# SyncE's order in the second entrance: slot 0's row and the fourth stack ahead of the second unit's writes, and the transposed maxima between two heads

## The reference

```
x = x + 0.5 * L0_ffn(ln(x)); x = x + L0_attn(ln(x)); x = x + 0.5 * L0_ffn(ln(x))
x = x + 0.5 * L1_ffn(ln(x)); x = x + L1_attn(ln(x)); x = x + 0.5 * L1_ffn(ln(x))

L1_attn: c_kv = x @ W_dkv.T ;  q = (x @ W_dq.T @ W_uq.T), 16 heads, times k_eff
         attn = softmax(causal(q_lat . c_kv / sqrt(8))) ;  y = (attn . c_kv) . v_eff
```

## Time and profile before

| what | value |
|---|---|
| median of 3 runs | 448.95 us (448.35 to 449.26) |
| the profiled execution: its own time | 450.93 us |
| its span in the profile | 448.8 us |
| TensorE busy | 404.5 us, 90% of the span |
| VectorE, ScalarE, GpSimd busy | 78%, 64%, 66% |
| DMA | 31.82 MB, mean 71 GB/s |

### The profile page before, as it was taken

One profiled execution on the slowest core, in us unless ns is written; L12 is line 12 of the kernel. 1 busy time (PEld: TensorE's weight loads), 2 busy tenths in 40 slices (PEclk: granted clock), 3 DMA queues, 4 the chain that ended last, 5 costly groups with the idle time before them and its releaser, 6 DMA issues.

```text
span 448.8 us, 11209 instructions
## 1 busy us (share of the span) xinstructions
PE 404.5 (90%) x3802; PEld 262.1 (58%) x3802; DVE 348.4 (78%) x878; ACT 286.1 (64%) x523; POOL 295.2 (66%) x557
## 2 busy tenths in 40 slices
PE   7999789999999998888879788879999999887996
PEld 2555436666666654444457564557777777545674
DVE  5888787887878866997799987747788888277992
ACT  6785525666676676787896447226558686778641
POOL 5524646777687772346999646346787789779962
PEclk9999999999999999999999999989999999999999
DMA  7001877332324200000000006895444331000001
GB/s 219 3 0 29 211 209 216 88 106 61 100 71 98 56 4 1 2 0 2 0 2 0 1 1 156 168 239 137 108 111 105 99 82 46 6 0 1 23 25 47
DMA packets 31124, 31.82 MB, mean 71 GB/s; under 512 B 4954, under 2 KB 26330, under 8 KB 31075
## 3 DMA queue, kind: packets, MB, share of 16 engines
q1 hardware_dynamic: 31074, 31.18, 27.3%
HBM read 21.30 MB, written 9.44 MB: 68 GB/s over the span
## 4 chain that ended last, share of the span: by engine, by line
PE 43%; DVE 20%; POOL 18%; issue 9%; ACT 5%; DMA 3%; SPq 1%; DVEq 0%; POOLq 0%; ACTq 0%
PE psum L725 5%; POOL hq L1523 4%; DVE nm L824 4%; PE psum L675 3%; POOL hb_v L1518 2%; POOL rstd L246 2%; PE psum L706 2%; PE psum L696 2%; PE psum L676 2%; PE psum L729 2%; DVE xn L240 2%; PE psum L678 2%; PE psum L697 2%; DVE stat L224 2%; PE psum L306 2%
## 5 line engine op out<-in xcount | busy, mean ns | idle before, releaser
L774 ACT ACTIVATE h_sb<-psum 128x1024 f32<-128x1024 f32 (+1 forms) x128 | 110.6, 914 | 54.1 <-PE psum L707 27.4
L824 DVE TENSOR_REDUCE nm<-psum 128x2 f32<-128x512 f32 x128 | 81.3, 683 | 11.9 <-PE psum L676 11.3
L827 DVE TENSOR_REDUCE nm<-psum 128x3 f32<-128x384 f32 x128 | 65.6, 551 | 15.4 <-PE psum L682 14.1
L784 POOL TENSOR_TENSOR h_sb<-h_sb,bandw 128x512 f32<-128x512 f32 x45 | 57.2, 1271 | 0.0
L246 POOL TENSOR_TENSOR rstd<-veps,mhalf 128x4 f32<-128x4 f32 (+1 forms) x25 | 26.2, 1049 | 43.7 <-DVE veps L232 43.2
L725 PE MATMUL psum<-h_sb,v_b 128*32 128x256 f32 x512 | 40.9, 391 | 3.9 <-POOL h_sb L788 2.1
L788 POOL TENSOR_SCALAR_AFFINE_SELECT h_sb<-h_sb 128x512 f32<-128x512 f32 x64 | 40.7, 637 | 0.0
L675 PE MATMUL psum<-kst,qst 72*128 72x256 bf16 x128 | 33.4, 278 | 3.2 <-DMA kst<-k_dram 1.4
L676 PE MATMUL psum<-kst,qst 72*128 72x256 bf16 x128 | 32.7, 272 | 0.0
L678 PE MATMUL psum<-kst,qst 72*128 72x128 bf16 x128 | 29.1, 228 | 2.5 <-DMA kst<-k_dram 1.8
L306 PE MATMUL psum<-h_sb,dw 128*64 128x256 f32 x256 | 30.9, 385 | 0.0
(11 more groups left out here) (256 smaller groups left out, 1144.4 us busy)
## 6 DMA issues: line engine op xcount, KB each, us to landing
qst<-q_dram SPq DMA_DIRECT2D x96, 96.0 KB
kst<-k_dram SPq DMA_DIRECT2D x96, 96.0 KB
q_dram<-q_parts SPq DMA_DIRECT2D x16, 192.0 KB, 3.0
k_dram<-k_parts SPq DMA_DIRECT2D x16, 192.0 KB, 2.9
k_dram<-k_parts SPq DMA_DIRECT2D x16, 128.0 KB, 3.2
x<-in_L_attn_x SPq DMA_DIRECT2D x4, 256.0 KB, 4.7
out_x<-x SPq DMA_DIRECT2D x4, 256.0 KB, 2.3
pk<-in_packed SPq DMA_DIRECT2D x1, 689.5 KB, 5.7
```

The source lines that it names most:

```text
L774: nc.scalar.activation(pexp[p][:, :, 0:w], psum[:, 4 + 2 * (p % 2):6 + 2 * (p % 2), 0:w], ACT.Exp, scale=scale).then_inc(sem("a_exp"), 1)
L784: ins = nc.gpsimd.tensor_tensor(wide, wide, bandw[:].unsqueeze(1).unsqueeze(1).to_broadcast([P, 2, 2, P]), ALU.mult)
L824: nc.vector.tensor_reduce(nm[slot % 2][:, HEAD[h]], bank[e].rearrange("p (t k) -> p t k", t=2), AX.X, ALU.max, negate=True).then_inc(sem(" ...
L827: nc.vector.tensor_reduce(nm3[slot % 2][:, HEAD[h]], bank[e][:, 0:3 * P].rearrange("p (t k) -> p t k", t=3), AX.X, ALU.max, negate=True).t ...
```

## The change

In the second entrance alone, SyncE no longer writes unit 1 ahead of row 0. It writes unit 1's first half behind stack 3, and its second half, then both halves of unit 2, then unit 3 behind row 1. In the second attention's front(1), TensorE's transposed maxima of slot 0 move from behind head 3 to between heads 2 and 3. For that `pe_scores` takes the heads of the pair that it is to do. The first layer's entrance keeps its order.

```
-            def pe_scores(pe, qd, slot, p, idle=0, b=6 if l0 else 5):
+            def pe_scores(pe, qd, slot, p, idle=0, b=6 if l0 else 5, which=range(2)):
...
-                for e in range(2):
+                for e in which:
...
                     for p in range(PR):
-                        pe_scores(eng, q0, slot, p, 1)
-                        if slot == 1 and p == 1:
+                        if slot == 1 and p == 1 and not l0:
+                            pe_scores(eng, q0, slot, p, 1, which=[0])
+                            pe_maxT(eng, q0, 0)
+                            pe_scores(eng, q0, slot, p, 1, which=[1])
+                        else:
+                            pe_scores(eng, q0, slot, p, 1)
+                        if slot == 1 and p == 1 and l0:
                             pe_maxT(eng, q0, 0)
...
                 at["prefetch"](eng, which)
-                run(ph, 3, 4 if which == "sp" else 5)
+                if which != "sp":
+                    run(ph, 3, 5)
+                elif ph is proj_a:
+                    run(ph, 3, 4)
...
                 elif which == "sp":
                     at["front"](eng, which, 0)
-                    ph["write"](eng, 2, [0])
+                    if ph is proj_a:
+                        ph["write"](eng, 2, [0])
+                    else:
+                        ph["write"](eng, 1, [0])
                     at["front"](eng, which, 1)
+                    if ph is proj_b:
+                        ph["write"](eng, 1, [1])
+                        ph["write"](eng, 2, [0])
                     ph["write"](eng, 2, [1])
                     ph["write"](eng, 3, [0, 1])
```

## The result

The changed kernel takes 455.92 us (median of 4 runs, 455.07 to 457.3) against 448.84 us of the kernel before: a ratio of 1.0161, 95% interval 1.0136 to 1.0186. The forecast was slower, 451.2 with a range up to 452.9. The side was right, the size was not: 7.1 us were lost where 2.2 were forecast.

What follows compares the result with a forecast made beforehand. TensorE was taken to bound the second attention. Unit 2 starting 0.9 us later for a late stack, plus 1.3 us of halved clock, made +2.2 us on the median of 448.95: 451.2 us, range 448.0 to 452.9.

Steps and rivals of the forecast that it cites:

- The bound: Second attention: TensorE is busy throughout, so its gains or losses before 308 us reach the end one to one.
- The row's wait goes: Second entrance: row 0, issued near 289.1, lands at 291.3, so TensorE's 2.46 us wait before slot 0's shifted scores goes.
- the sum: Whole kernel: unit 2 starts 0.9 us later and the clock costs 1.3, together +2.2 us, giving 451.2.
- rival A: Unit 2: the stack comes in time and the gain stands, 446.4 to 448.0 us; chance 0.12.
- The next transposition waits for the split: Second entrance: the second transposition needs slot 1's split and runs at 293.4 instead of 294.75, a gain of 1.35 us.
- The late stack: Unit 2: the next quad's stack, issued at 302.6, lands at 309.2 (308.3 to 310.3), starting the unit 0.9 us later.
- The clock: Behind unit 2's pause of 3.5 us TensorE's clock is halved, costing 1.3 us, bounds 0 and 1.7.
- Rivals B and A: B, a draw at unit 2: stack lands 308.3 to 309, 448.1 to 449.8 us, chance 0.2; A has its own line.
- Rival D: Second attention: row 1 or row 2 is late too, two pauses, up to +5 us; chance 0.08.

Runs made afterwards that it cites:

- e9: The kernel before, unchanged, run again for a second profile; ratio 1.0004 to the kernel before.
- e1: The kernel before with only the transposed maxima moved between heads 2 and 3, SyncE's order kept; ratio 0.998 to the kernel before.
- e2: The kernel before with only SyncE's new order, the transposed maxima staying behind head 3; ratio 1.0152 to the kernel before.
- e5: The whole change, but unit 1's six writes are issued by ScalarE on its own queue; ratio 0.9978 to the kernel before.
- e8: The whole change, but unit 1's first half is written ahead of row 0 again, its second where the first stood; ratio 1.0063 to the kernel before.
- e4: The whole change, but the writes of units 2 and 3 go behind stack and row in units 1 to 3 of the first quad; ratio 1.0068.
- e6: The whole change, but the writes of units 2 and 3 are spread over units 1 and 3 of the first and second quads; ratio 0.9984.
- e3: The whole change plus 19 filler matmuls on TensorE ahead of unit 2's first scores; ratio 1.010 to the kernel before.
- e7: The whole change plus 9 filler matmuls on TensorE ahead of unit 2's first scores; ratio 1.0104 to the kernel before.

## Why the prediction was right in its side and wrong in its size

*The bound: right.* All of the difference lies in TensorE's stretch and reaches the end, to 0.1 us.

*The row's wait goes: right for this profile, but it was no property of the kernel.* No wait stands at 291.84. But e9 has 0.39 of the 2.46 us, and e1 none, with the writes ahead. I took one execution for the rule, and the half-clock stretch behind the wait with it. In the sum this hardly counts, as unit 2 swallows any gain; for rival A and for what the change could ever win it does.

*The next transposition waits for the split: right,* 293.83 for 293.4. Unit 2 was reached at 306.19 (310.41 less 4.22) for 305.7, 0.5 us short.

*The late stack: right in kind, too small in size.* It was issued at 304.42 where the sum gave 302.6: row 0 went out 0.4 later, a half took 1.6 to 1.7 instead of 1.55, and one issue took 1.41 (at 298.49) instead of 0.5. It landed at 310.36 where the sum gave 309.2 and its upper bound 310.3 (which by its own terms, 309.2 and 1.0, should read 310.2). As a delay of unit 2 that is 2.0 us for 0.9. e2, e5 and e8 bear out the cause: the issues moved behind the row, and the hole in the queue that they left. The hole alone does no harm (e4 and e6), but how the two share the delay no run shows; from 301 to 305 the queue was full (a share of 1.04) while SyncE was still issuing. The rule of the Trainium skill that I weighed (DMA: Bandwidth & Descriptors, Why a DMA increments its semaphore by 16 and not by 1) agrees with the trace again: while stacks moved with no writes beside them, from 282 to 288, the engines' share was 0.80, near 12 of 16. But the sum missed the hole itself: three microseconds with a share of 0.17. It had put it at 0.2 us, because it took stack 2 to be in flight until 290.8 as before. In the changed kernel stack 2's last packets end at 289.1 and its last semaphore event is at 289.88, and then nothing moves until row 0's packets at 290.9. The writes beside it had not held it: from its first issue to its landing stack 2 took 7.7 us in e1 and in e9, with the writes, and 8.9 with the change, without them. The 11.0 us of the first profile (279.74 to 290.77) belonged to that execution, as did the row's wait.

*The clock: the term that failed.* I put it at 1.3 us, bounded by 1.7. The figures came from the one low stretch in the trace, 3.4 us. The cost measured 4.50, as the clock stayed down for 10.2 us with TensorE busy throughout. Against the 2.2 forecast for the stretch, 6.5 came: 3.2 of the 4.3 between are the clock, 0.7 the longer wait, 0.5 the smaller lead (rounded). The clock alone is 2.8 us past its upper bound, the stack's landing only 0.1. The bound was wrong in kind: the length of one low stretch behind one pause was taken as the most that a longer pause can cost. That the clock would fall at all was forecast rightly, and e3 shows that the pause is what brings it down.

*Rivals B and A,* the draw and the gain, fell with the pause. Rival D put a second pause beside the first; none came, SyncE's rows were in time.

## What to carry to other kernels

Idle time of a queue and of the engine that issues to it is worth keeping filled, if the list behind it is full: work moved out of the idle stretch comes back there one for one (1.64 us of issuing per half-unit here). Before paying for a wait seen in one profile, look whether a second profile of the same kernel has it. And price a pause of TensorE by the pause and by a stretch at half clock behind it that can be longer than the pause (10.2 us behind 4.2 here). If the pause can't be removed, filler over most of it (4.3 of 5.3 us) gave some 3 us back here.

## What the runs showed of the hardware

The low clock's length isn't set by the pause's length alone. Behind pauses of 0.4 to 1.1 us (e5, e3 behind its filler, e9) there was none. Behind 1.8 (e4) it was 6.8 us, behind 2.3 (e8) 3.4, behind 2.46 (before) 3.4, behind 4.2 (the change) 10.2, behind 4.8 (e7) 13.6, and behind 5.7 (e2) 6.8, all read in windows of 1 us. In e2 and e7 about 2 us of it lay in the pause itself; otherwise TensorE was busy again all the while. Nor does a pause of one length always bring it: ahead of the second entrance, near 254 us, TensorE idles 1.50 us for the same GpSimd result in each of these kernels. In e4 and e6 the clock is halved for 10.2 us behind that; in the kernel before and in the change it stays at 1.00.

The time of a stack's transfer, from its first issue to the matmul that it releases, also varied: 5.4 us in e5, 5.6 in e9, 6.0 with the change, 6.8 in e2, 7.2 in e3 and 8.6 in e7, with the same bytes. In e3 and e7 the last few semaphore events alone were late, as said there; what makes the rest vary stays open.
